# Low score products of a graph attention layer as pairs of 64 rows behind one another

## The reference

```python
q = x @ wq.T + bq
k = x @ wk.T + bk
v = x @ wv.T + bv
q2 = (q @ wiq.T + biq).reshape(N, H, D).transpose(1, 0, 2)
k2 = (k @ wik.T + bik).reshape(N, H, D).transpose(1, 0, 2)
v2 = (v @ wiv.T + biv).reshape(N, H, D).transpose(1, 0, 2)
mask = _build_mask(edge_index, edge_type, edge_type_weights, x.dtype)
scores = jnp.einsum('hnd,hmd->hnm', q2, k2) * scale + mask[None]
attn = jax.nn.softmax(scores, axis=-1)
out = jnp.einsum('hnm,hmd->hnd', attn, v2)
out = out.transpose(1, 0, 2).reshape(N, OUT_F)
return out @ wo.T + bo
```

## Time and profile before

| what | value |
|---|---|
| median of the runs | 299.97 us |
| the profiled execution | 299.66 us |
| its span, first to last instruction | 297.9 us |
| TensorE busy in it | 289.7 us |
| VectorE busy | 200.7 us |
| ScalarE busy | 175.8 us |
| GpSimd busy | 142.5 us |
| mean granted clock of TensorE | 0.997 |
| start of the first steady pair step used below | 207.42 us |

### The profile page before, as it was taken

One profiled execution on the slowest core, in us unless ns is written; L12 is line 12 of the kernel. 1 busy time (PEld: TensorE's weight loads), 2 busy tenths in 40 slices (PEclk: granted clock), 3 DMA queues, 4 the chain that ended last, 5 costly groups with the idle time before them and its releaser, 6 DMA issues.

```text
span 297.9 us, 5259 instructions
## 1 busy us (share of the span) xinstructions
PE 289.7 (97%) x1640; PEld 274.0 (92%) x1640; DVE 200.7 (67%) x494; ACT 175.8 (59%) x330; POOL 142.5 (48%) x124
## 2 busy tenths in 40 slices
PE   8999899999999999999998999999999999999992
PEld 8999899999999998888998999999999998887882
DVE  4869967677666764204458798888888888843184
ACT  5863244323443352221299899999999999934432
POOL 2000635535556452659953445545463637845600
PEclk9999999999999999999999999999999999999998
DMA  7978556363662448826210404030312121410013
GB/s 219 379 251 310 178 177 211 108 181 135 207 217 79 134 141 320 315 73 185 105 41 31 142 0 143 12 130 25 116 47 94 59 82 70 150 64 0 2 70 141
DMA packets 14318, 39.83 MB, mean 134 GB/s; under 512 B 3200, under 2 KB 4832, under 8 KB 14176
## 3 DMA queue, kind: packets, MB, share of 16 engines
q1 hardware_dynamic: 12192, 38.38, 37.7%
q0 software_dynamic: 1680, 0.62, 1.1%
q10 hardware_dynamic: 432, 0.66, 0.8%
HBM read 37.44 MB, written 2.21 MB: 133 GB/s over the span
## 4 chain that ended last, share of the span: by engine, by line
PE 89%; DVE 5%; ACT 4%; issue 1%; DVEq 0%; ACTq 0%
PE bank L897 21%; PE bank L888 17%; PE bank L890 17%; PE bank L889 17%; PE bank L994 6%; PE bank L977 5%; PE bank L963 2%; PE bank L967 2%; PE bank L906 2%; DVE res L664 1%; ACT probs L486 1%; ACT w_hi L393 1%; ACT L486 0%; DVE w_lo L600 0%; DVE h_lo L790 0%
## 5 line engine op out<-in xcount | busy, mean ns | idle before, releaser
L336 POOL DMA_INDIRECT mask_cells<-cell_value,cell x48 | 54.9, 1143 | 75.0 <-DMA mask_cells<-cell_value,cell 31.0
L307 POOL TENSOR_TENSOR w_lo<-w_raw,w_hi 128x1024 fp32r<-128x1024 f32 x20 | 47.6, 2403 | 44.1 <-DVE probs L783 40.2
L888 PE MATMUL bank<-x_hi,w_hi 128*128 128x384 f32 x192 | 64.4, 336 | 0.8 <-DVE h_lo L682 0.8
L393 ACT ACTIVATE w_hi<-w_raw 128x1024 fp32r<-128x1024 f32 x50 | 52.4, 1054 | 20.8 <-PE bank L897 19.6
L889 PE MATMUL bank<-x_lo,w_hi 128*128 128x384 f32 x192 | 64.2, 334 | 0.0
L890 PE MATMUL bank<-x_hi,w_lo 128*128 128x384 f32 x192 | 64.2, 334 | 0.0
L440 ACT ACTIVATE h_hi<-bank,bcol 128x384 f32 (+1 forms) x24 | 14.0, 582 | 58.1 <-PE bank L890 58.1
L888 PE MATMUL bank<-h_hi,w_hi 128*128 128x384 f32 x128 | 46.4, 362 | 0.0
L600 DVE TENSOR_TENSOR w_lo<-w_raw,w_hi 128x1024 fp32r<-128x1024 f32 x30 | 36.6, 1222 | 12.5 <-ACT w_hi L393 10.1
L890 PE MATMUL bank<-h_hi,w_lo 128*128 128x384 f32 x128 | 43.0, 336 | 0.0
L889 PE MATMUL bank<-h_lo,w_hi 128*128 128x384 f32 x128 | 42.9, 335 | 0.0
(11 more groups left out here) (103 smaller groups left out, 530.2 us busy)
## 6 DMA issues: line engine op xcount, KB each, us to landing
w_raw<-weights SPq DMA_DIRECT2D x54, 512.0 KB, 3.3
probs<-key_rows SPq DMA_DIRECT2D x6, 512.0 KB, 3.8
res<-x_rows SPq DMA_DIRECT2D x1, 1536.0 KB, 6.8
out<-res SPq DMA_DIRECT2D x6, 256.0 KB, 2.0
v<-x_t SPq DMA_DIRECT2D x6, 192.0 KB, 5.7
w_raw<-weights SPq DMA_DIRECT2D x3, 256.0 KB, 5.8
mask_cells<-cell_value,cell POOLq DMA_INDIRECT x48
mask_cells<-mask SPq DMA_DIRECT2D x1, 576.0 KB, 4.1
```

Of the source, the lines that this page charges most:

```text
L307: nc.gpsimd.tensor_tensor(lo, w_raw[:, s, cols], hi.bitcast(F32), ALU.subtract)\
L336: nc.gpsimd.indirect_dma_start(out=mask_cells, out_offset=bass.IndirectOffsetOnAxis(ap=cell[:, c:c + 1], axis=0), in_=cell_value[:, c:c + ...
L393: nc.scalar.activation(w_part(t, s, slice(0, F))[0], w_raw[:, s, :], ACT.Copy).then_inc(w_hi_done, 1)
L888: pe.matmul(out_ps, w_hi[:, s, cols], moving_hi, start=(k == 0), stop=False)
```

## The change

`SCORE_PLACES` becomes (2, 3, 4): the blocks' high products stand one k earlier. The low products are taken out of `scores` and put into a function of their own, `low_scores`, which runs once per pair behind the high products of block 2. Its six products contract over 64 rows only, the head's own half of q's low part with that half of k; the heads alternate, rows 0 to 63 and 64 to 127. The zero halves and the tile `q_more` go, and with them the clearing. For this all six row tiles are open at once and get banks of their own, 0 to 5. Banks 4 and 5 are also `out_bank`, so block 2 waits for `sum_done` of the pair before, and VectorE's `add_halves(a - 1, 1)` moves ahead of the masks. Row tiles are masked, raised and divided in the order 0, 2, 4, 1, 3, 5. The transposes use banks 0, 2, 1 in place of 0, 2, 3. In the tail, blocks 0 and 1 follow each other, the first wait of block 1 of the output projection is for three masks of the pair, and the sixth mask stands behind `normalise` there too.

```diff
-SCORE_PLACES = (3, 4, 5)
+SCORE_PLACES = (2, 3, 4)
...
-        q_more = sb("q_more", [P, 2, N], F32R)
-        q_low = (h_hi[:, V0 + 7, :], h_lo[:, V0 + 7, :]), (q_more[:, 0, :], q_more[:, 1, :])
+        q_low = h_hi[:, V0 + 7, :], h_lo[:, V0 + 7, :]
...
-        score_bank = [bank[i] for i in (0, 1, 2, 3, 0, 1)]
+        score_bank = bank[0:6]
+
+        ROW_TILES = (0, 2, 4, 1, 3, 5)
...
-            return bank[(0, 2, 3)[g % 3]]
+            return bank[(0, 2, 1)[g % 3]]
...
-            def exps(a, tiles=range(2 * NT)):
-                for i in tiles:
-
-                    act.wait_ge(masked, 2 * NT * a + (i + 1))
+            def exps(a, places=range(2 * NT)):
+                for place in places:
+                    i = ROW_TILES[place]
+
+                    act.wait_ge(masked, 2 * NT * a + (place + 1))
...
-            for slot in range(2):
-                for h in range(2):
-                    nc.vector.memset(q_low[slot][h][(1 - h) * D:(2 - h) * D, :].bitcast(F32), 0.0)
...
-                last = u is None
-                for i in range(6 if last else 5):
-                    mask_scores(a, i)
-
-                normalise(a, (0, 2))
-                normalise(a, (4,))
-                if not last:
-                    mask_scores(a, 5)
-                normalise(a, (1, 3))
+                if not (isinstance(a, int) and a == 0):
+                    add_halves(a - 1, 1)
+                for place in range(5):
+                    mask_scores(a, place)
+                normalise(a, (0, 1))
+                normalise(a, (2,))
+                mask_scores(a, 5)
+                normalise(a, (3, 4))
                 pt_low(a, (0,))
                 normalise(a, (5,))
                 pt_low(a, (1,))
-                if not (isinstance(a, int) and a == 0):
-                    add_halves(a - 1, 1)
                 pt_low(a, (2,))
...
-                if b == 2:
-
-                    pe.wait_ge(masked, 2 * NT * a + 2)
-
+                if b == NT - 1 and not (isinstance(a, int) and a == 0):
+
+                    pe.wait_ge(sum_done, 2 * a)
                 for h in range(2):
 
                     pe.matmul(score_bank[2 * b + h][:, 0:N], q_high[:, 2 * par + h, q], k_parts[:, 2 * par + h, :],
                               start=True, stop=False)
-                for h in range(2):
-
-                    pe.matmul(score_bank[2 * b + h][:, 0:N], q_low[par][h][:, q], k_parts[:, 2 * par + h, :],
-                              start=False, stop=True).then_inc(scores_ready, 1)
+
+            def low_scores(a, par):
+                for b in range(NT):
+                    q = slice(b * P, (b + 1) * P)
+                    for h in range(2):
+
+                        here = slice(h * D, (h + 1) * D)
+                        pe.matmul(score_bank[2 * b + h][:, 0:N], q_low[par][here, q], k_parts[here, 2 * par + h, :],
+                                  start=False, stop=True).then_inc(scores_ready, 1)
...
+                            if k == SCORE_PLACES[-1]:
+                                low_scores(a, 1 - par)
...
             scores(a, 1, 0)
+            scores(a, 1, 1)
             project(0, 0, right)
-            scores(a, 1, 1)
             project(0, 1, right)
             scores(a, 1, 2)
+            low_scores(a, 1)
             project(0, 2)
 
-            pe.wait_ge(masked, 2 * NT * PAIRS - 1)
+            pe.wait_ge(masked, 2 * NT * PAIRS - 3)
```

More of the change, by code:

```diff
@@ L749, in evacuate_pair @@
                     here, there = slice(h * D, (h + 1) * D), slice((1 - h) * D, (2 - h) * D)
-                    low = k_parts[there, 2 * slot + h, :] if which else q_low[slot][h][here, :]
+                    low = k_parts[there, 2 * slot + h, :] if which else q_low[slot][here, :]
                     ins = nc.vector.scalar_tensor_tensor(
@@ L765, in add_halves, with mask_scores @@
                     .then_inc(sum_done, 1)
-            def mask_scores(a, i):
+            def mask_scores(a, place):
+                i = ROW_TILES[place]
                 dve.wait_ge(scores_ready, 2 * NT * a + (i + 1))
@@ L775, in mask_scores, with normalise @@
                                                accum_out=neg_max[:, i:i + 1]).then_inc(masked, 1)
-            def normalise(a, tiles):
-                dve.wait_ge(exp_done, 2 * NT * a + (tiles[-1] + 1))
+            def normalise(a, places):
+                dve.wait_ge(exp_done, 2 * NT * a + (places[-1] + 1))
+                tiles = [ROW_TILES[place] for place in places]
                 cols = slice(tiles[0], tiles[-1] + 1, 2)
```

## The result

| | before | changed |
|---|---|---|
| median of the runs | 299.97 us | 310.81 us (310.53 to 311.21) |
| ratio, 95% interval | | 1.0367 [1.0354, 1.038] |
| profiled execution, its span | 299.66, 297.9 us | 310.62, 308.8 us |
| TensorE busy | 289.7 us (97%) | 294.0 us (95%) |
| granted clock | 0.997 | 0.995 |

The change makes the kernel 3.7% slower. One of the four executions of the kernel before took 1647.63 us, for a reason that stays open; neither the median nor the ratio rests on it. 311.0 was forecast, with 306.5 to 315.0 as the range.

What follows compares the result with a forecast made beforehand. TensorE was taken to bound the kernel, busy 289.7 of 297.9 us. Second pair +1.1, five loops 6.75, tail 2.5, seven D 0.7 make +11.05: 299.66 to 310.7, plus 0.3 for the median, 311.0; range 306.5 to 315.

Steps and rivals of the forecast that it cites:

- the closed loop: Steps after the first full one: exp 0 waits for ScalarE's last att_half copy; period 15.90 us + D against 14.55.
- D: Cost of changing TensorE's mode before the low products: taken as 0.10 us, bounds 0 to 0.16, counted seven times.
- the tail: After the pair steps: waits for sum_done and the late sixth mask make transposes later; +2.5 us taken, D besides.
- The chain to the first mask: In a step, att_half copy, add, TensorE wake, scores, mask: first mask at S+6.01+D (S: step's start), 1.9 us later.
- The wait at block 2: TensorE waits before the third block for sum_done's add of the previous pair: a stall of 0.59 us per step.
- The saving: Six low products become three pairs on TensorE: 0.52 us less per pair of heads, 4.15 us over eight.
- The second wait: TensorE waits at a step's transposes for VectorE's normalised tiles: 0.85 us.
- The first pair: No sum_done wait there; mask 1.6 us later, but transposes were already held back by table load and exps: 0.
- Only the first wait counts: Rival: VectorE under 3.1 us from mask to tile, ScalarE's work below 12.4, no loop; 303.7 us, chance 0.07.
- Mode changes are dear: Rival: each change costs a whole product's latency, 0.33 us, and as much again behind the low products; 313.5 us, chance 0.10.
- Pairs do not overlap: Rival: the six low products still take six times 0.173 us, only the tail pays, +0.5; 311.5 us, chance 0.12.
- The wait is covered and the saving arrives: Rival: att_half copy ends by S+3.75 (S: step's start), add done when the third block comes; 295.8 us, chance 0.03.

Runs made afterwards that it cites:

- The copy first: Changed kernel, with ScalarE copying the odd head's att_half before the split and the copy of v: 307.72 us, ratio 1.0275.
- Masks first in the tail: Changed kernel, with the sixth mask put ahead of the normalised tiles in the tail alone, as before the change: 309.28 us, ratio 1.0319.

## Why the prediction was right, point by point

**Its two waits and the closed loop** are there, in the places that it named. Not by median alone: the pair steps were to lose 8.45 us by the sum (1.1, 5 x 1.35, six D) and lost 8.49; the tail was to lose 2.6 with its D and lost 2.4. That the sum came within 0.2 us of the median is in part luck: several of its terms were off by 0.2 to 0.5 us and cancelled, as follows.

**The chain to the first mask.** Copy to add to TensorE: forecast 0.64, measured 217.00 - 216.35 = 0.65. VectorE from mask to transposes: forecast 3.94, measured 3.92. The wait at block 2 was to be 0.59 and is 0.39 in a step, since TensorE gets there later than forecast: block 0 starts 2.97 us into the step (214.78 - 211.80) and not 2.71, held by the k2 eviction, and its two products take 0.45. The loop did not depend on it, as its wait ends when VectorE's add does.

**The loop** was forecast at 15.90 + 0.10 and measured at 15.93. Two errors hide in that. ScalarE's work was taken as 13.68 and is 13.50. An idle time shown on ScalarE costs more than it says: from the second split to the sixth exp it was 1.25 us between starts (215.16 to 216.41) with 0.20 idle shown, and is 0.95 now (221.80 to 222.75), where the exp starts 0.09 before the split is shown to end. So the two idle times that vanished, 0.46 together, were worth more than the 0.46 and 0.1 that I took off. The rest was taken as 2.22 + 0.10 and is 2.43, since a change of mode delays the first scores twice, 0.10 before the first low product and 0.10 in it. They nearly cancel. The first such step was to lose 1.1 + D and lost 1.39, as much as the others.

**D** was the wrong idea of the price. It was bounded at 0 to 0.16 by "the pipeline empties". The whole price is 0.40 us on TensorE, 0.20 going in and 0.20 coming out, and 0.19 on the path to the scores, above the bound of 0.16. As TensorE was waiting anyway, only the 0.19 was paid in the steps, seven times 0.1 more than forecast. The forecast said that the way out was covered by the wait for the transposes. That held: the run without a pairing, whose low block is longer and whose scores are earlier, waits there 0.27 us in place of 0.60.

**The saving**, taken as 0.52 us a pair of heads, is 0.11: (0.10 + 0.72 + 0.11) against 1.04. It was the largest wrong term, and it did not show because the forecast had it covered too. In the earlier trace rows nothing could tell it, as no product of before contracts over 64 rows. Its products over 64 columns do not show such a price: one starts at 219.11, 0.18 after the full product before it, and the next product 0.18 after it. Whether they count as a change of mode no run shows, so the forecast's "no run of before changes the mode" is open.

**The second wait** was forecast at 0.85 and is 0.60. From block 2 on, TensorE takes 4.50 us to the transposes (217.00 to 221.50) where 4.08 was forecast, 0.3 of it in the low block and 0.1 on the way into it; the tiles take 5.10 where 4.92 was forecast.

**The tail**: 2.5 and D forecast, 2.4 measured. Counted from the tail's start (251.09 before, 259.58 now), the wait for the sixth mask ends at 11.79 where 11.71 + D was forecast, and two errors cancel in it: the first mask comes at 7.40 where 6.92 + D was forecast, and the three normalised tiles take 1.5 us where the earlier trace rows had 1.9. The wait itself is 1.16 and not 1.9, because TensorE comes to it 0.7 us later than forecast: block 2 starts 0.28 later (at 6.22, not 5.94), and the products behind three masks another 0.3. A wait of 0.33 for a weight tile's low part, which the forecast did not have, lies ahead of block 2's. Moving the mask gave back 1.5.

**The first pair**: forecast 0, measured 158.32 against 158.18. The 0.14 says nothing: in the traces of "The copy first" and "Masks first in the tail", which differ from the changed kernel only behind this place, the same row stands at 158.21 and 158.59.

**The rivals.** "Only the first wait counts" falls by its own conditions, 3.92 us and not under 3.1 on VectorE and 13.50 and not under 12.4 on ScalarE. "Mode changes are dear" was nearer than the forecast on TensorE's bill, 0.40 where it had 0.66 for both ways, and wrong on the kernel's. "Pairs do not overlap" fell with the pairs in place. "The wait is covered and the saving arrives" asked for an att_half copy that ends by 3.75 us into a step; with the copy first it ends at 3.37 (213.12 + 0.48 - 210.23), and the kernel is still 2.7% slower than before.

## What to carry to other kernels

Two instructions that run side by side are worth what they save after the change of mode is paid: here 0.40 us around each stretch, more than two full products of 384 columns, so three pairs in a stretch save 0.11 us of TensorE's time and one pair loses 0.22; and even the three lost 1.06 us over the kernel, since their first result comes 0.19 us later. To gather work for that puts its results late and lets them fall in behind whatever owns the banks: before such a change, follow the first result to the engine that waits for it, and see whether a new wait leads back into the list of an engine that has no rest. A fixed order can make an engine with a 59% share of the span the bound.

## What I had not expected of the hardware

A change of mode costs about the same in either direction: the next product starts 0.10 us late going into 64-row products and 0.09 coming out, and on either side the first product in the new mode is shown 0.44 us long where 0.33 is usual and is followed after 0.28 in place of 0.17, much like the refill after a wait. The expectations' 0.20 for the way out had a refill in it. No kernel of this study is faster than the one before: the best, with low products of full height gathered behind k = 3, is at 0.9996 [0.9987, 1.0005], which is no difference.
